# Vision tower on one core: scores from 16-bit high and low parts, and a convolution that looks one plane ahead

## The reference, cut to what matters

```python
# convolution ("token") stage, per channel, 31 x 31 taps
result = conv(image, normalized_template)
std = sqrt(boxmean(image * image) - boxmean(image) ** 2)
tokens = where(isnan(r), 0, r) with r = (result / (std + 1e-9)).mean(channels)
# attention: 16 query heads, 8 key heads of 64, 256 tokens an image
q = l2norm(x @ Wq) * (q_gamma + 1) * 8 ; k = l2norm(x @ Wk) * (k_gamma + 1) * 8
sim = tanh(q @ k.T / 50) * 50 / 8, causal softmax, @ v, @ Wout, + tokens, layer norm
# multilayer: silu(x w1) * (x w2), two gelu layers, w3, + x, layer norm
```

## Time and profile before

| | us |
|---|---|
| median of 3 runs | 1901.03 (1897.28 to 1901.47) |
| the profiled execution | 1905.45, its span 1903.6 |
| PE busy | 1789.2 (94%) |
| DVE busy | 1109.4 (58%) |
| ACT busy | 870.3 (46%) |
| POOL busy | 424.4 (22%) |

### The profile page before, as it was taken

How to read it: one execution, slowest core, us unless ns; L and a number is a source line. 1 busy time by engine, 2 the same in 40 slices (tenths; PEclk the granted TensorE clock), 3 DMA queues, 4 the chain that set the end, 5 groups by cost and what they waited for, 6 DMA issues and landing times. The chain is left out here.

```text
span 1903.6 us, 31322 instructions
## 1 busy us (share of the span) xinstructions
PE 1789.2 (94%) x11640; PEld 1554.9 (82%) x11640; DVE 1109.4 (58%) x1964; ACT 870.3 (46%) x1073; POOL 424.4 (22%) x516
## 2 busy tenths in 40 slices
PE   5988999999988999998999999899999999999998
PEld 4888998988976877787787788778888888888886
DVE  8788888888766565676557575343241423414142
ACT  4655544555525674676477477322221222222221
POOL 2000000000020221222122122143433434434342
PEclk9989999999988999999999999899999999999999
DMA  5321222224101000200200010350000000000000
GB/s 171 119 81 73 81 106 74 81 81 147 54 34 60 24 16 10 91 23 17 83 24 20 26 54 24 108 191 23 1 23 0 22 0 22 22 0 23 1 12 13
DMA packets 26344, 96.79 MB, mean 51 GB/s; under 512 B 3033, under 2 KB 11353, under 8 KB 20962
## 3 DMA queue, kind: packets, MB, share of 16 engines
q1 hardware_dynamic: 26210, 94.96, 14.6%
HBM read 82.33 MB, written 24.15 MB: 56 GB/s over the span
## 5 line engine op out<-in xcount | busy, mean ns | idle before, releaser
L586 PE MATMUL conv<-w_hi,x_hi 128*128 128x368 f16 (+5 forms) x1320 | 355.7, 279 | 7.9 <-issue 6.0
L586 PE MATMUL conv<-w_lo,x_hi 128*128 128x368 f16 (+5 forms) x1320 | 356.6, 279 | 0.0
L586 PE MATMUL conv<-w_hi,x_lo 128*128 128x368 f16 (+5 forms) x1320 | 355.2, 279 | 0.0
L1354 ACT ACTIVATE raw_c<-ring,sh 128x512 f32<-128x512 f32 x128 | 87.5, 689 | 334.4 <-PE ring L1457 334.3
L864 POOL TENSOR_SCALAR_AFFINE_SELECT probs<-probs 128x256 f32<-128x256 f32 x256 | 123.9, 508 | 435.2 <-ACT probs L940 435.2
L1142 PE MATMUL mixed<-v,probs 128*128 128x65 f32 x1536 | 198.7, 280 | 15.6 <-DVE o L1024 12.0
L1142 PEld LDWEIGHTS mixed<-v,probs 128*128 128x128 f32 x1536 | 182.4, 193 | 32.0 <-issue 17.5
L1366 DVE CAST ha_hi<-raw_c 128x512 fp32r<-128x512 f32 x128 | 90.6, 708 | 201.0 <-ACT raw_c L1354 198.8
L1313 POOL TENSOR_TENSOR ha_lo<-raw_c,ha_hi 128x512 fp32r<-128x512 f32 x128 | 165.3, 1291 | 187.8 <-DVE ha_hi L1366 187.8
L586 PEld LDWEIGHTS conv<-w_hi,x_hi 128*128 128x128 f16 x1320 | 193.2, 146 | 16.9 <-issue 8.5
L1457 PE MATMUL ring<-ha_hi,wh 128*128 128x512 f32 x512 | 199.6, 390 | 0.9 <-POOL ha_lo L1313 0.9
(11 more groups left out here) (147 smaller groups left out, 3491.0 us busy)
## 6 DMA issues: line engine op xcount, KB each, us to landing
xt<-x_columns_in SPq DMA_DIRECT2D x12, 1163.0 KB, 5.6
xp<-x_patches_in SPq DMA_DIRECT2D x12, 1152.0 KB, 5.2
hidden_words<-hidden_weights_in SPq DMA_DIRECT2D x8, 1408.0 KB, 9.0
words<-hidden_words SPq DMA_DIRECT2D x32, 352.0 KB, 3.0
wh<-hidden_words SPq DMA_DIRECT2D x8, 1024.0 KB, 10.0
tokens<-planes SPq DMA_DIRECT2D x4, 1024.0 KB, 4.3
lines<-tokens SPq DMA_DIRECT2D x4, 1024.0 KB, 5.6
h<-tokens SPq DMA_DIRECT2D x4, 1024.0 KB, 6.9
```

The costliest lines, as they stand in the source:

```text
L586: ins = pe.matmul(out, xs[:, c, RI - 1 - i:RI - 1 - i + NR, :, x].rearrange("p r g -> p (r g)"), w, start=(t == 0), stop=(t == len(terms) ...
L1354: act.activation(raw[:, u % 4], bank, ACT.Gelu, scale=scale[:, m:m + 1]).then_inc(s_gelu, 1)
```

## The change

Two parts, both in hand-written orders.

Convolution: every engine's body now works one plane ahead. DVE does sum_across(n, 1), variance(n), both sum_down of n + 1, inverse(n), split_lo(n + 1), three scalings, sum_across(n + 1, 0) and the fourth scaling. PE turns the sums of n + 1 behind the third and the fourth bank. PE's first group goes into the loop.

Scores: queries times the product of the gammas, and keys times 8, are each split into a 16-bit high part (ACT) and a low part (DVE, the exact value less the high part); a score is high x high, high x low and low x high. The gammas are first divided by their largest magnitude over 4096, or by 1 if that is larger (`fold_span`, with a maximum over partitions on POOL), and tanh's scale takes the factor back. Keys are stored once for two heads, without gamma.

```diff
...
+KEY_SCALE = 8.0
+GAMMA_SPAN = 4096.0
...
-                load_xt(0, 2, 2)
 
             def body(g, c, n, last):
                 if not (last and c >= 1):
+                    load_xt(*after(*after(g, c)), n + 2)
                     load_x(*after(*after(g, c)), n + 2)
-                if not last:
-                    load_xt(g + 1, c, n + CHANNELS)
                 if c < 2:
                     size = P // GROUPS // 2
...
+            pool.wait_ge(sh.s_gamma, 6)
+            pool.partition_all_reduce(sh.span[:, 1:2], sh.span[:, 0:1], P, bass.bass_isa.ReduceOp.max)\
+                .then_inc(sh.s_span, 1)
...
             def body(g, c, n, last):
-                if not (last and c == 2):
+                more = not (last and c == 2)
+                turned(n, 1)
+                mean_square(n)
+                if more:
                     split_hi((c + 1) % CHANNELS, n + 1)
-                if not (last and c >= 1):
-                    square(n + 2)
-                if not (last and c == 2):
+                    square(n + 1)
+                deviation(n)
+                if more:
+                    regroup(n + 1, 0)
+                    regroup(n + 1, 1)
                     turned(n + 1, 0)
-                    turned(n + 1, 1)
-                    mean_square(n + 1)
-                if not (last and c >= 1):
-                    regroup(n + 2, 0)
-                    regroup(n + 2, 1)
-                if not (last and c == 2):
-                    deviation(n + 1)
...
+                dve.tensor_scalar(sh.gq[:], sh.gamma[:], -1.0, None, ALU.mult).then_inc(sh.s_gamma, 1)
+                dve.wait_ge(sh.s_gamma, 4)
+                dve.tensor_tensor(sh.gq[:], sh.gq[:], sh.gamma[:], ALU.max).then_inc(sh.s_gamma, 1)
+                dve.wait_ge(sh.s_gamma, 5)
+                dve.tensor_reduce(sh.span[:, 0:1], sh.gq[:], AX_X, ALU.max).then_inc(sh.s_gamma, 1)
+
+            def fold_span():
+                dve.wait_ge(sh.s_span, 1)
+                dve.tensor_scalar(sh.span[:, 2:3], sh.span[:, 1:2], 1.0 / GAMMA_SPAN, 1.0, ALU.mult, ALU.max)\
+                   .then_inc(sh.s_gamma, 1)
+                dve.wait_ge(sh.s_gamma, 7)
+                dve.reciprocal(sh.span[:, 3:4], sh.span[:, 2:3]).then_inc(sh.s_gamma, 1)
+                dve.wait_ge(sh.s_gamma, 8)
+                dve.tensor_scalar(sh.gamma[:], sh.gamma[:], sh.span[:, 3:4], 1.0 / KEY_SCALE, ALU.mult, ALU.mult)\
+                   .then_inc(sh.s_gamma, 1)
+                dve.tensor_scalar(sh.span[:, 2:3], sh.span[:, 2:3], 1.0 / CLAMP, None, ALU.mult).then_inc(sh.s_gamma, 1)
+                dve.wait_ge(sh.s_gamma, 10)
...
-                sum_down(1, 0)
-                sum_across(0, 1)
-                variance(0)
-                sum_down(1, 1)
                 dve.wait_ge(s_tpad, 32)
 
             def body(g, c, n, last):
-                more, more_down = not (last and c == 2), not (last and c >= 1)
+                more = not (last and c == 2)
+                sum_across(n, 1)
+                variance(n)
+                if more:
+                    sum_down(n + 1, 0)
+                    sum_down(n + 1, 1)
+                else:
+                    fold_weights()
                 dve.wait_ge(s_part, n * 4 + 4)
                 inverse(g, c, n)
-                if last and c == 2:
-                    fold_weights()
                 if more:
                     split_lo((c + 1) % CHANNELS, n + 1)
-                if more_down:
-                    sum_down(n + 2, 0)
-                scale(g, c, n, 0)
+                for b in range(3):
+                    scale(g, c, n, b)
                 if more:
                     sum_across(n + 1, 0)
-                if more_down:
-                    sum_down(n + 2, 1)
-                scale(g, c, n, 1)
-                if last and c == 2:
+                else:
                     scale_tokens()
-                if more:
-                    sum_across(n + 1, 1)
-                    variance(n + 1)
-                scale(g, c, n, 2)
+                    fold_span()
                 scale(g, c, n, 3)
 
...
-                turn_sums(0, range(4))
-                correlate(0, 0, 0)
-                turn_sums(0, range(4, 8))
-                correlate(0, 0, 1)
-                correlate(0, 0, 2)
-                turn_sums(1, range(4))
-                correlate(0, 0, 3)
-                turn_sums(1, range(4, 8))
-                for c in range(1, CHANNELS):
-                    body(0, c, c, False)
+                turn_sums(0, range(8))
 
             def body(g, c, n, last):
-                correlate(c, n, 0)
-                if not (last and c == 2):
+                more = not (last and c == 2)
+                for b in range(3):
+                    correlate(c, n, b)
+                if more:
                     turn_sums(n + 1, range(4))
-                correlate(c, n, 1)
-                if not (last and c == 2):
+                correlate(c, n, 3)
+                if more:
                     turn_sums(n + 1, range(4, 8))
-                correlate(c, n, 2)
-                correlate(c, n, 3)
-
-            planes(pe, body, first, 1)
+
+            planes(pe, body, first)
...
-        qt = sb("qt", [P, 2, HEADS, TOK])
-        kt = sb("kt", [P, 2, HEADS, TOK])
+        q_hi = sb("q_hi", [P, 2, HEADS, TOK], F16)
+        q_lo = sb("q_lo", [P, 2, HEADS, TOK], F16)
+        k_hi = sb("k_hi", [P, 2, EB, TOK], F16)
+        k_lo = sb("k_lo", [P, 2, EB, TOK], F16)
...
-                            act.activation(qt[:, img % 2, 4 * r:4 * r + 4, P * (tb - 2):P * (tb - 1)],
-                                           bank.rearrange("p (h t) -> p h t", t=P), ACT.Copy)\
-                               .then_inc(s_emptied["queries"], 1)
+                            for e in range(4):
+                                u = 4 * r + e
+                                ins = act.activation(q_hi[:, img % 2, u, P * (tb - 2):P * (tb - 1)], bank[:, e * P:(e + 1) * P],
+                                                     ACT.Copy, scale=gamma[:, u:u + 1])
+                            ins.then_inc(s_qkhi, 1)
+                        else:
+                            bank = read_out(run, g, step)
+                            act.wait_ge(s_score, m * HEADS + 8)
+                            act.activation(k_hi[:, img % 2, :, P * (tb - 2):P * (tb - 1)],
+                                           bank.rearrange("p (h t) -> p h t", t=P), ACT.Copy, scale=KEY_SCALE)\
+                               .then_inc(s_qkhi, 1)
                     elif kind == "score":
                         n = step[1]
                         act.wait_ge(s_score, g * NH + n + 17)
                         act.wait_ge(s_mix, g * NH + n + 13)
                         act.activation(probs[:, n % 4], sim[:, n % 2, :, 0:3 * P], ACT.Tanh,
-                                       scale=1.0 / CLAMP).then_inc(s_tanh, 1)
+                                       scale=sh.span[:, 2:3]).then_inc(s_tanh, 1)
...
-                    elif kind == "make" and step[2] >= 8 and step[2] % 4 >= 2:
-                        img, tb = step[1], step[2] // 4 - 2
-                        bank = read_out(run, g, step).rearrange("p (h t) -> p h t", t=P)
-                        dve.wait_ge(s_score, image(g, img) * HEADS + 8)
-                        for m in range(2):
-                            by = gamma[:, m::2].rearrange("p (h t) -> p h t", t=1).to_broadcast([P, EB, P])
-                            ins = dve.tensor_tensor(kt[:, img % 2, m::2, P * tb:P * tb + P], bank, by, ALU.mult)
-                        ins.then_inc(s_emptied["keys"], 1)
+                    elif kind == "make" and step[2] >= 8:
+                        img, tb, r = step[1], step[2] // 4 - 2, step[2] % 4
+                        cols = slice(P * tb, P * tb + P)
+                        bank = read_out(run, g, step)
+                        dve.wait_ge(s_qkhi, image(g, img) * 6 + 3 * tb + r + 1)
+                        if r < 2:
+                            for e in range(4):
+                                u = 4 * r + e
+                                ins = dve.scalar_tensor_tensor(out=q_lo[:, img % 2, u, cols], in0=bank[:, e * P:(e + 1) * P],
+                                                               scalar=gamma[:, u:u + 1], in1=q_hi[:, img % 2, u, cols],
+                                                               op0=ALU.mult, op1=ALU.subtract)
+                            ins.then_inc(s_emptied["queries"], 1)
+                        else:
+                            dve.scalar_tensor_tensor(out=k_lo[:, img % 2, :, cols], in0=bank.rearrange("p (h t) -> p h t", t=P),
+                                                     scalar=KEY_SCALE, in1=k_hi[:, img % 2, :, cols],
+                                                     op0=ALU.mult, op1=ALU.subtract).then_inc(s_emptied["keys"], 1)
...
-                            for m in range(2):
```

(11 more changed lines are left out.)

13 lines of the change are left out of this document (5 added, 8 removed).

## The result

| | before | after |
|---|---|---|
| median, us (6 runs each) | 1901.25 (1897.28 to 1904.51) | 1919.5 (1911.83 to 1936.34) |
| ratio, 95% interval | | 1.0107 (1.0074 to 1.014) |
| span of the profiled execution, us | 1903.6 | 1934.6 |
| mean granted clock over the span | 0.973 | 0.957 |

The change costs about 20 us by the ratio (14 to 27), 18.3 by the medians. The forecast was 1907 with a range of 1881 to 1925, slower with 0.57. The time lies inside that range, but outside the band of the forecast itself (1898 to 1914). The profiled execution of the changed kernel is the slowest of its six, and its six mean clocks run from 0.957 (1936.34 us) to 0.973 (1911.83 us), with a median of 0.967; so its rows show mechanisms, and sizes are taken from medians where the two differ.

What follows compares the result with a forecast made beforehand. PE was taken to pace attention, with DVE level twice an image, and DVE to pace the convolution. Terms -27.7 + 28 + 6 = +6.3 on the 1901.03 us median gave 1907, range 1881 to 1925.

Steps and rivals of the forecast that it cites:

- the forecast itself: Whole kernel: the summed terms hold and the time is 1898 to 1914 us; chance 0.42.
- Convolution, -27.7 forecast: Convolution stage: DVE's 5.8 us wait a plane goes, PE paces, stage ends at 528.4; gain 27.7 us, bounds 15 to 34.
- The tail: Convolution's end: last scaling behind scale_tokens and late POOL subtractions; +2 us, bounds 0 and +9.
- (c): Convolution: gains only half, DVE late in valid-mask planes and the tail long; total 1921 us, chance 0.09.
- (d): Convolution: another wait replaces the one for ACT, gain 0 to 5 us; total 1932 us, chance 0.04.
- (b): Scores: 16-bit halves don't run side by side, or skill's rule holds; score 0.95 to 1.0, total 1917 us, chance 0.18.
- the 0.17 for going in and out of the halves: Scores: about 0.17 us added to 0.51 of products, making a score 0.68 us instead of 0.86.
- Rival (a): Attention evictions: ACT and DVE at their lower bounds, attention +9 us, clock 0; total 1882 us, chance 0.27.
- forecast +1.4: Attention, one image: mix net +0.55 us and next image's first score +0.85, together +1.4 although every score is faster.
- The clock, +6 with bounds 0 and 12: Attention: clock falls behind new PE waits in half the images, 8 x 1.2 us, partly swallowed by DVE's next wait; +6.
- the queue term: Attention: new evictions in ACT's and DVE's in-order queues delay mix and keys; +28 us, bounds +9 and +45.
- the sum for attention: Attention: +28 us for eviction delays, net of faster scores, and +6 for the clock.

Runs made afterwards that it cites:

- convolution alone: The convolution's new order with queries, keys and scores as in the kernel before: 1873.34 us, 0.9853 against the kernel before.
- products alone: The changed kernel with the old evictions written in 16 bits and the low parts left out, three 16-bit products kept: 1883.69 us, 0.9901 against the kernel before.
- one pass: The changed kernel with queries' high part in one ACT pass and low part in one DVE pass, without gammas: 1893.81 us, 0.9967 against the kernel before.
- later jobs: The changed kernel with an image's jobs reordered and moved between heads, same instructions: 1903.91 us, 1.0013 against the kernel before.
- fourth pass: The changed kernel with the high-by-high product issued twice in each score: 1926.46 us, 1.0142 against the kernel before.
- evictions alone: The changed kernel with its new evictions kept, but scores from the old 32-bit products: 1935.19 us, 1.0175 against the kernel before.
- best order: Convolution's new order, PE's first group outside the loop, old scores and evictions, image jobs moved around the reductions: 1846.93 us, 0.9735 against the kernel before.
- the scores alone: The 16-bit scores, two evictions and scaled gammas in the old convolution order: 1946.89 us, 1.0236 against the kernel before.

## Why the prediction was right

**An account.** For each kernel: the median less that of the convolution alone; the span lost to the clock (span times one less the mean granted clock; for the changed kernel the median 0.967 of its six clocks); an image at full clock (first score to first score, second to third image of a group); and what the last two give together, an estimate, (lost - 29.9) + 16 x (image - 34.2).

| kernel | against 1873.3 | idle of PE, first score to last mix | lost to clock | image | account |
|---|---|---|---|---|---|
| convolution alone | 0 | 29.5 | 29.9 | 34.2 | 0 |
| products alone | +10.4 | 43.1 | 56.4 | 32.8 | +4 |
| one pass | +20.5 | 52.2 | 56.7 | 33.4 | +14 |
| later jobs | +30.6 | 55.2 | 57.0 | 34.0 | +24 |
| changed kernel | +46.2 | 74.7 | 63 | 35.0 | +46 |
| fourth pass | +53.1 | 64.7 | 55.7 | 35.9 | +53 |
| evictions alone | +61.9 | 55.6 | 61.8 | 36.3 | +66 |
| best order | -26.4 | 20.9 | 22.1 | 33.8 | -14 |

It holds within 7 us where the scores or evictions were touched; the best order gains 12 us more than it says, and 6 of them are its shorter multilayer stage. With the median clock of every kernel in place of the profiled one, the changed kernel's clock term is 63 - 34 = 30 us instead of 33.

**Convolution, -27.7 forecast:** 25.7 in the profile, 28.1 for the part alone. The mechanism is right step by step: first product 27.56 (27.7), last start 521.99 (523.5), period 41.0 (40.9), DVE's wait for the root gone, DVE waiting for banks, two holes of 2.25 and 1.96 us (2.1 each). The tail was mis-sized: from the last product to the stage's end 8.4 us, +5.5 and not +2, and by POOL's stand before the reduction, not by its subtractions. It lies inside the bounds of 0 to 9. That the part alone came out at 28.1 is partly luck: it has no maximum at its end, its last scaling ends at 523.4 where it ended at 555.5, and the multilayer stage, which the forecast put at nothing, took about 5 us of that back. Rivals (c) and (d), with half the gain or none, fall.

**Scores.** 0.60 us (0.68 forecast), so the halves do run side by side in 16 bits, and rival (b) falls. The six pairs take the 0.51 worked out; the 0.17 for going in and out of the halves, for which the prediction had no row, is 0.09. The Trainium skill's "TensorE: Matmul & The Clock Gate", section "Back-to-back issue gap", has about 81 ns a product for such a stream. Twelve products here take from 809.44 to 809.95 (the last pair starts at 809.89, and a pair of its width takes 0.06), 43 ns each on average, because two half-height products run at a time; the measurement decides, and the rule does not hold for this form.

**Evictions.** ACT's four 1.13 us (1.1), DVE's four 1.13 (1.1), keys 0.68 (0.65), tanh 902 ns (811 + 90): all as worked out (the prediction's slope of 0.83 ns a column is 0.87 by its own two rows, which moves the pass by 0.01). Waits for the reading of mixed 42.3 us (35 to 50), for keys 6.4 (10). Rival (a), light evictions, falls: its point was four passes under 0.9 us. An image at full clock costs +0.8 us, forecast +1.4; the faster scores give back more inside the image than I had counted. That is 13 us over sixteen images, forecast 28. An image that also prepares a new group costs more, as forecast: in the second and third group it took 40.57 us at clock 0.92 and 38.99 at 0.96 where the convolution alone took 35.84 and 35.82 at full clock, so about 1.5 at full clock instead of 0.8, and the term is nearer 15.

**The clock, +6 with bounds 0 and 12, is the step that failed.** By the account it is about 30 to 33 us, well outside; that is an estimate, and no experiment holds the waits and varies the clock. I had counted only the new waits, each once, with a drop behind half of them. The runs show a price that does not follow single waits: products alone, with the slower tanh, put only 14 us more idle time into PE and lost 26 us to the clock. What held the total inside the range is luck: the queue term was too large by some 13 to 15 us and the clock term too small by 24 to 27; the sum for attention was 34 and is 46. With the convolution's 28 that gives +18, inside the range and slower, as said. It is 12 us above the 1907 of the sum and nearer to what (b) and (c) gave, 1917 and 1921, by neither of their mechanisms. The total was right in sign by a mechanism of which I had the smaller half.

**What stays open.** In these profiles the clock was 0.98 to 1.00 with 21 to 30 us of PE's idle time between first score and last mix, and 0.92 to 0.96 with 43 to 75. Why 43 us already cost nearly as much as 75 is not shown; how the idle time is spread may count, and no run here varied that alone. Of the 10.4 us that products alone add, no run tells what tanh's pointer does; an experiment with the old scores and only that pointer would. The account's split, too, is arithmetic and not an experiment, since more waits and less clock come together. The first stretch of attention and the group boundaries are in neither term, and the scores alone leave 12 us to them.

## What to carry to other kernels

When PE sets the pace by a hair, a gain in its own work can be lost again to the clock: products alone saved 1.4 us an image at full clock and the kernel got slower. Price the clock by an experiment before building the operand splitting, and let it change nothing else; here it also carried tanh's pointer and a longer end of the convolution. Count an added eviction by who is queued behind it on each in-order engine, and look for the place in the order before the instruction: the same work in another order was worth 16 us here, and moving the reductions behind the query jobs in the old kernel 18 us. Split a change that has two independent parts and time each; here one part gained 28 us and hid that the other lost 45.

## What was not expected of the hardware

- POOL stood 5.69 us before the maximum over the partitions, with nothing to wait for in the profile, and then ran it in 0.38 us.
- PE's loop in the convolution leaves a hole of 2.0 to 2.3 us each time round in the profile of the changed kernel. Where PE's first group stood in that loop, PE had two more holes, 3.1 to 3.7 us together, in the multilayer stage, in nine profiles of nine; where it stood outside, none in five of five.
- Two 16-bit products on half the rows each, side by side, follow the pair before them at 0.11 us (256 columns) and 0.06 us (128 columns), as fast as a full-height product.
- The mean clock of one kernel varied from 0.957 to 0.973 between six executions, and its time with it, by 24.5 us. The convolution alone kept its time within 5 us in five executions, but the kernel before, in 17 of one set, went from 1894.64 to 1922.21.
